# Other slot numbers in the order tables of a decoder layer (attention, eight experts, ternary layer) on one core

## The chip, the cores and the metric

The kernel runs on one core of a Trainium2 chip. The metric is the device time of the core in microseconds (us). Five engine programs run side by side and meet at semaphores: PE (TensorE, matmuls and transposes), DVE (VectorE), ACT (ScalarE), POOL (GpSimd) and SP (SyncE, which issues the DMAs). PEld in the profile is PE's weight loads. PE's clock has two levels, 1.2 and 2.4 GHz; the profile gives the granted clock as a share of full speed.

## The reference

Sixteen batches of 128 tokens with 256 features go through one post-norm layer (cut to what matters):

```
def attn(x):                       # 16 heads of 16
    scores = q k^T / 4, causal
    vals, idx = top_k(scores, 32)  # the 32 largest of each row stay
    return (softmax(masked scores) @ v) Wo^T + bo
def xattn(x, ctx, itok):           # 8 experts, 256 -> 512 -> 256
    h = relu(proj_in[e] @ x);  o = proj_out[e] @ h
    gate[b, s, e] = sum of ctx[b, s, k] where itok[b, s, k] == e
    return sum over e of gate[e] * o[e]
def ffn(x):                        # Hadamard, 4 bits, ternary weight
    return quantize4(x @ H) @ ternary(weight)^T
x = layernorm(x + attn(x)); x = layernorm(x + xattn(x)); x = layernorm(x + ffn(x))
```

## The kernel before, in words

**Units.** The work is cut into 8 units of 2 batches (256 tokens). Each unit passes through steps: q, k and v projections; four score tiles k = 0..3 (scores, copy_scores and exp, first_max, select, keep, turn_probs twice, copy_probs, attend, normalise; a tile is 8 heads of one batch); turn_o, copy_ot, out_proj; ln1_stats, rstd1, ln1_apply, turn_x1 and the two copies x1t_high and x1t_low; the 8 experts; the second layernorm, turn_x2, hadamard, quantise, turn_q4, ffn; the third layernorm and the store. Below, step.index@unit names one of them: L1.0.1@3 is the first expert matmul of expert 0, half 1, in unit 3.

**Experts.** Each is two products with weights and activations split into a high and a low 16-bit part, three matmuls a product. L1.e.z (line 752, 12 matmuls) computes half z of the 512 hidden values of expert e into ps_z; ACT's relu writes h_hi (line 576) and h_raw (line 580); POOL's h_low (line 462) is the difference of the two. L2.e.b (line 768, 12 matmuls) takes all hidden values of batch b, so it waits for h_low of both halves. ACT's gate_out scales the result and POOL's gated_add sums it up. PE's order of experts is L1.0.0, L1.0.1, L1.1.0, L2.0.0, L1.1.1, L2.0.1, and so on: the first L2 of an expert stands one L1 behind the second half of it.

**Weight preparation.** In the first unit each expert's weights are read from HBM (load_w, two buffers), squared and summed (w_squares on ACT, w_sum on PE at line 778), given a power-of-two scale by w_scale (DVE, lines 931 to 944), and split by w_high (ACT, lines 607 and 609) and w1_low and w2_low (POOL, lines 471 and 474). L1 and L2 of unit 0 wait for these.

**One bank.** q, k, v, attend, turn_o, out_proj, turn_x1, turn_x2, hadamard, turn_q4 and ffn all write the PSUM tile ps_misc; each waits (take_misc, table MISC) until the reader of the one before it in PE's order has read it. So which step waits for which reader follows from the order.

**The order.** It is written out by numbers. `build_schedule` gives each step of each unit a slot: unit v starts at 32 v, the steps of a tile have an offset from 8 k + shift_k, experts run one step a slot from `at["experts"]`. The steps are sorted by slot (ties stay in the order of placing), and `walk` lets each engine run its own steps in that order. Four tables hold the numbers: FIRST for unit 0, SECOND for unit 1, STEADY for units 2 to 6, LAST for unit 7; PREP and PREP_SLOTS place the weight preparation. The semaphore waits belong to the steps and go with them.

```
        at = FIRST if v == 0 else SECOND if v == 1 else LAST if v == UNITS - 1 else STEADY
        base = SLOTS * v
    return [step for _, step in sorted(placed, key=lambda x: x[0])]
```

As slots of unit v + 1 run from 32 (v + 1) and the experts of unit v from 32 v + 44, the score tiles and attends of the next unit lie among the experts of this one.

Of the kernel before, what the change touches and what calls it, by code (L numbers as in the profile page):

```python
# [111 lines left out]
}  # L112
FIRST = STEADY | {
    "experts": 42.5, "shift1": 1.5, "relu": 0.5, "gate_out": 3, "shift2": 0.5, "copy_ot": 38.5, "shift0": 3,
    "select": 3.75, "copy_scores": -3.75, "copy_v": 10.5, "shift3": -0.5, "out_proj": 40, "turn_probs2": 10.5,
    "gate_scale": 48.5, "gated_add": 2, "pace": 0.875, "x_plus_bo": 27, "scores": -3.75, "rstd2": 76.75, "v": 10,
    "keep": 6.5, "ffn_residual": 86.25, "ln2_stats": 77.5, "spread_q": -4.75, "rstd1": 38.25, "k": -6.25,
    "x2t_high": 77.75, "load_ctx": 20.25, "copy_probs": 8, "attend": 12.25, "gate_sums": 31.5, "turn_probs": 8.75,
# [914 lines left out]
```

How the kernel before makes its waits and increments, by code:

```python
        def wait(eng, s, value):  # L368
            if value > 0:
                eng.wait_ge(s, value)
# [4 lines left out]
        @block.sync  # L376
# [9 lines left out]
            def step(name, v, *args):  # L386
# [10 lines left out]
                        .then_inc(s_ctx, 16)  # L397
                    sp.dma_start(itok_sb[:, :, :], itok.rearrange("b s k -> s b k")[:, v * UB:(v + 1) * UB, :])\
                        .then_inc(s_ctx, 16)
                elif name == "load_w":
                    e, = args
                    wait(sp, w1_low_ready, e - STAGED + 1)
                    wait(sp, w2_low_ready, e - STAGED + 1)
                    sp.dma_start(w1_raw[:, e % STAGED, :, :], rows(w1t[e])).then_inc(w_loaded[e % STAGED], 16)
                    sp.dma_start(w2_raw[:, e % STAGED, :, :], rows(w2t[e])).then_inc(w_loaded[e % STAGED], 16)
                elif name == "store":
                    sp.wait_ge(out_ready, v + 1)
                    sp.dma_start(out.rearrange("b s d -> s b d")[:, v * UB:(v + 1) * UB, :], out_sb[:, :, :])\
                        .then_inc(s_store, 16)
            sp.dma_start(wq_sb[:, :, :], rows(wqt)).then_inc(s_qk, 16)
            load_xt(0)
# [6 lines left out]
            sp.dma_start(wo_sb[:, :, :], rows(wot)).then_inc(s_vo, 16)  # L419
            sp.dma_start(bv_sb[:, :], bv[:, :]).then_inc(s_vo, 16)
            sp.dma_start(bo_sb[:, :], bo.rearrange("(a n) -> a n", a=1).broadcast_to([P, D])).then_inc(s_vo, 16)
            sp.sem_inc(s_store, 16)
            walk("sp", step, sp)
            sp.wait_ge(s_store, 16 * (UNITS + 1))
```

## Time and profile before

| | |
|---|---|
| median of three runs | 622.8 us (622.05 to 624.53) |
| the profiled execution, own time | 624.53 us |
| its span, first to last instruction | 622.7 us |
| mean granted clock of PE | 0.941 |
| busy, share of the span | PE 89%, PEld 77%, DVE 77%, ACT 62%, POOL 55% |
| L1 and L2 matmuls (lines 752 and 768) | 3072 of PE's 7156 instructions, 273 to 274 ns each |

A row of a timeline has the start in us from the start of the span, the duration, the engine, the line, the operation with output and inputs, and in square brackets the idle time of the engine before it with what released it. Matmuls overlap (a new one starts every 0.11 us, each takes 0.27), so the ends of PE's rows are modelled. "<-issue" means that the profile shows nothing that was waited for. The rows themselves stand in a section of their own, in numbered groups.

### The profile page before, as it was taken

To read this page: it belongs to the slowest core of one execution; us is meant where nothing else is said; L and a number is where in the kernel's file an instruction comes from. 1 tells how busy PE (TensorE), PEld (TensorE's weight loads), DVE (VectorE), ACT (ScalarE), POOL (GpSimd) and SP (SyncE) were. 2 spreads that over 40 slices of the span, in tenths; PEclk is the share of its full clock that TensorE was granted. 3 is DMA by queue.
4 is the path that set the end of the run, shared out by engine and by line. 5 is a ranking of instruction groups with operands and counts; after the bars stand their busy time and mean duration, and the time that the engine had idled before them with its cause. 6 is when DMAs were issued, how large, how long until landed. Compare 5 with 4: busy or idle time off the path is not lost. (4 is left out here: it accounts for less than half of the span.)

```text
span 622.7 us, 20334 instructions
## 1 busy us (share of the span) xinstructions
PE 553.3 (89%) x7156; PEld 478.9 (77%) x7156; DVE 477.5 (77%) x2995; ACT 387.2 (62%) x909; POOL 344.3 (55%) x336
## 2 busy tenths in 40 slices
...
PEclk9568578999999999999999999999999999999985
...
GB/s 234 78 146 136 86 103 2 3 17 37 3 2 3 64 8 2 3 3 69 3 1 21 53 3 2 3 70 1 3 3 53 3 3 1 19 0 3 18 0 17
DMA packets 20021, 19.88 MB, mean 32 GB/s; under 512 B 1744, under 2 KB 17872, under 8 KB 19920
## 3 DMA queue, kind: packets, MB, share of 16 engines
...
HBM read 16.49 MB, written 2.10 MB: 30 GB/s over the span
## 5 line engine op out<-in xcount | busy, mean ns | idle before, releaser
L462 POOL TENSOR_TENSOR h_lo<-h_raw,h_hi 128x512 f16<-128x512 f32 x128 | 149.5, 1169 | 158.9 <-ACT h_raw L580 158.2
L768 PE MATMUL ps_o<-w_hi,h_lo 128*128 128x256 f16 x512 | 139.8, 273 | 4.3 <-POOL h_lo L462 3.1
L752 PE MATMUL ps_z<-x1t_hi,w_lo 128*128 128x256 f16 x512 | 140.5, 274 | 0.6 <-DVE x1t_lo L910 0.6
L752 PE MATMUL ps_z<-x1t_lo,w_hi 128*128 128x256 f16 x512 | 140.3, 274 | 0.0
L752 PE MATMUL ps_z<-x1t_hi,w_hi 128*128 128x256 f16 x512 | 140.3, 274 | 0.0
L768 PE MATMUL ps_o<-w_hi,h_hi 128*128 128x256 f16 x512 | 139.5, 273 | 0.0
L768 PE MATMUL ps_o<-w_lo,h_hi 128*128 128x256 f16 x512 | 139.5, 273 | 0.0
L854 DVE MATCH_REPLACE8 taken<-next,taken 128x48 f32<-128x48 f32 (+2 forms) x576 | 127.6, 233 | 0.2
L576 ACT ACTIVATE h_hi<-ps_z 128x512 f16<-128x512 f32 x128 | 75.9, 593 | 57.9 <-PE ps_z L752 57.0
L849 DVE MAX8 next<-taken 128x8 f32<-128x48 f32 (+2 forms) x576 | 95.9, 235 | 0.1
L483 POOL TENSOR_TENSOR acc<-go_sb,acc 128x512 f32<-128x512 f32 x56 | 71.2, 1271 | 36.4 <-ACT go_sb L590 36.2
L580 ACT ACTIVATE h_raw<-ps_z 128x512 f32<-128x512 f32 x128 | 76.0, 593 | 0.0
L590 ACT ACTIVATE go_sb<-ps_o,gate 128x256 f32<-128x256 f32 x128 | 53.7, 474 | 25.0 <-PE ps_o L768 24.9
L768 PEld LDWEIGHTS ps_o<-w_hi,h_lo 128*128 128x128 f16 x512 | 50.0, 98 | 13.2 <-POOL h_lo L462 5.2
L553 ACT ACTIVATE pt_sb<-ps_pt 64x512 f32<-64x512 f32 x64 | 38.0, 593 | 35.4 <-PE ps_pt L714 35.3
L752 PEld LDWEIGHTS ps_z<-x1t_hi,w_lo 128*128 128x128 f16 x512 | 50.4, 98 | 7.5 <-DVE x1t_lo L910 1.0
L768 PEld LDWEIGHTS ps_o<-w_lo,h_hi 128*128 128x128 f16 x512 | 50.1, 98 | 7.1
L752 PEld LDWEIGHTS ps_z<-x1t_lo,w_hi 128*128 128x128 f16 x512 | 50.4, 98 | 6.7
L752 PEld LDWEIGHTS ps_z<-x1t_hi,w_hi 128*128 128x128 f16 x512 | 50.4, 98 | 6.0
L768 PEld LDWEIGHTS ps_o<-w_hi,h_hi 128*128 128x128 f16 x512 | 50.1, 98 | 5.8
L545 ACT ACTIVATE ps_s<-s_sb,neg_max 128x48 f32<-128x48 f32 (+2 forms) x192 | 51.5, 317 | 0.0
L714 PE MATMUL ps_pt<-ident,p_sb 128*128 128x128 f32 x256 | 42.5, 292 | 9.5 <-DVE p_sb L863 5.7
...
## 6 DMA issues: line engine op xcount, KB each, us to landing
...
```

The costliest lines, as they stand in the source:

```text
L462: nc.gpsimd.tensor_tensor(h_lo[:, e % 2, 2 * z:2 * z + 2, :], h_raw[:, z, :, :], h_hi[:, e % 2, 2 * z:2 * z + 2, :], ALU.subtract)\
L483: nc.gpsimd.tensor_tensor(acc[:, :, :], go_sb[:, e % 2, :, :], prev[:, :, :], ALU.add)\
L545: last = act.activation(dst, s_sb[:, k % 2, score_at(j):score_at(j) + m], ACT.Exp, bias=neg_max[:, k % 2, j:j + 1], scale=SCALE)
L553: act.activation(pt_sb[0:rows, k % 2, :, HALF * half:HALF * (half + 1), :].rearrange("p h j q -> p j h q"), ps_pt[0:rows, :].rearrange("p ...
L576: act.activation(h_hi[:, e % 2, 2 * z:2 * z + 2, :], ps_z[z][:, :].rearrange("p (c t) -> p c t", c=2), ACT.Relu)\
L580: act.activation(h_raw[:, z, :, :], ps_z[z][:, :].rearrange("p (c t) -> p c t", c=2), ACT.Relu)\
L590: last = act.activation(go_sb[:, e % 2, b, :], ps_o[e % 2][:, b * D:(b + 1) * D], ACT.Copy, scale=gate[:, b, e:e + 1])
L714: last = pe.transpose(ps_pt[:, i * P:(i + 1) * P], p_sb[:, k % 2, at:at + P], ident[:, :])
L752: last = pe.matmul(ps_z[z][:, d * UT:(d + 1) * UT], w[:, e, c, at:at + P], x[:, c, :], start=n == 0, stop=n == len(terms) - 1)
L768: last = pe.matmul(ps_o[e % 2][:, b * D:(b + 1) * D], h[:, e % 2, c, b * SEQ:(b + 1) * SEQ], w[:, e, c, :], start=n == 0, stop=n == len(te ...
L849: last = V.max(next8[:, j, :], t)
L854: last = V.match_replace(t, next8[:, j, :], t, TAKEN)
```

## The change

Only numbers in the tables change, in all four of them and in PREP; PREP_SLOTS goes from 6.0 to 5.5. Every step, instruction, buffer and semaphore is the same, and so is the work of each engine. What changes is the order of the steps within PE, DVE, ACT, POOL and SP. Of the tables, some numbers:

```diff
 STEADY = {
-    "shift0": 1.25, "shift1": 0, "shift2": 1.5, "shift3": -1, "scores": -6.5, "copy_scores": -6.25, "exp": 5.25,
-    "select": 2, "pace": 1, "keep": 7.25, "turn_probs": 8.5, "copy_probs": 8.25, "turn_probs2": 10,
-    "copy_probs2": 9.75, "attend": 11.75, "normalise": 12.75, "load_xt": 10, "q": -14, "copy_q": -13.25,
...
+    "shift0": 1.25, "shift1": 0, "shift2": 1.5, "shift3": -0.75, "scores": -5.75, "copy_scores": -6, "exp": 5,
+    "select": 1.75, "pace": 1.625, "keep": 7.25, "turn_probs": 8.25, "copy_probs": 8, "turn_probs2": 9.25,
+    "copy_probs2": 8.75, "attend": 10.75, "normalise": 12.75, "load_xt": -0.25, "q": -12.75, "copy_q": -13.5,
...
-PREP_SLOTS = 6.0
+PREP_SLOTS = 5.5
 PREP = {
-    "load_w": 10.75, "w_squares": 0.25, "w_sum": 2.25, "w_scale": 3.75, "w_high": 3.5, "w1_low": 3.75, "w2_low": 5.5,
-    "ffn_abs": -6.25, "ffn_sum": 26, "ffn_ternary": 42.25,
+    "load_w": 2, "w_squares": -0.75, "w_sum": 1.5, "w_scale": 3, "w_high": 1.75, "w1_low": 6.5, "w2_low": 9.75,
+    "ffn_abs": 14.25, "ffn_sum": 19, "ffn_ternary": 43.5,
 }
```

What this does to the order is seen in three places. First PE in unit 3, at the first expert (units 2, 4 and 5 have the same rows; within a group of twelve matmuls only the first is shown). Before, with attend.0 of unit 4 (L725) behind L1.0.1 (ps_z1):

```order
L752 MATMUL ps_z0<-x1t_hi,w1_lo 128x256 [waits relu_done,x1t_low]
...
L752 MATMUL ps_z1<-x1t_hi,w1_lo 128x256 [waits relu_done]
...
L725 MATMUL ps_misc<-v_sb,pt_sb 64x17 [waits v_copied,pt_copied,x1t_low]
...
L752 MATMUL ps_z0<-x1t_hi,w1_lo 128x256 [waits relu_done]
...
L768 MATMUL ps_o0<-w2_hi,h_lo 128x256 [waits go_done,h_low_done]
```

And after:

```order
L752 MATMUL ps_z0<-x1t_hi,w1_lo 128x256 [waits relu_done,x1t_low]
...
L725 MATMUL ps_misc<-v_sb,pt_sb 64x17 [waits v_copied,pt_copied,x1t_low]
...
L752 MATMUL ps_z1<-x1t_hi,w1_lo 128x256 [waits relu_done]
...
L752 MATMUL ps_z0<-x1t_hi,w1_lo 128x256 [waits relu_done]
...
L768 MATMUL ps_o0<-w2_hi,h_lo 128x256 [waits go_done,h_low_done]
```

The attend moved from behind L1.0.1 to ahead of it, so only L1.0.1 and L1.1.0 are left between L1.0.1's start and L2.0.0.

Second PE in the start, where q@1 (L636) stands among the steps of unit 0 (L725 attend, L714 turn_probs, L778 w_sum, L695 scores). Before:

```order
L778 MATMUL ps_o0<-w_sq,ones 128x2 [waits w_step,w_squared]
L725 MATMUL ps_misc<-v_sb,pt_sb 64x17 [waits v_copied,pt_copied]
L725 MATMUL ps_misc<-v_sb,pt_sb 64x17 x15
L636 MATMUL ps_misc<-xt_sb,wq_sb 128x256 [waits xt_loaded,o_ready]
L636 MATMUL ps_misc<-xt_sb,wq_sb 128x256 x3
L714 MATMUL ps_pt<-ident,p_sb 128x128 [waits pt_copied,p_ready]
L714 MATMUL ps_pt<-ident,p_sb 128x128 x3
L695 MATMUL ps_s<-kt_sb,q_spread 32x16 [waits s_copied,s_zeroed,p_ready,spread_ready,k_copied]
```

And after:

```order
L778 MATMUL ps_o0<-w_sq,ones 128x2 [waits w_step,w_squared]
L725 MATMUL ps_misc<-v_sb,pt_sb 64x17 [waits v_copied,pt_copied]
L725 MATMUL ps_misc<-v_sb,pt_sb 64x17 x15
L714 MATMUL ps_pt<-ident,p_sb 128x128 [waits pt_copied,p_ready]
L714 MATMUL ps_pt<-ident,p_sb 128x128 x3
L636 MATMUL ps_misc<-xt_sb,wq_sb 128x256 [waits xt_loaded,o_ready]
L636 MATMUL ps_misc<-xt_sb,wq_sb 128x256 x3
L714 MATMUL ps_pt<-ident,p_sb 128x128 [waits pt_copied,p_ready]
L714 MATMUL ps_pt<-ident,p_sb 128x128 x3
L778 MATMUL ps_o0<-w_sq,ones 128x2 [waits w_step,w_squared]
L695 MATMUL ps_s<-kt_sb,q_spread 32x16 [waits s_copied,s_zeroed,p_ready,spread_ready,k_copied]
```

q@1 moved behind a turn_probs, and w_sum.3 stands ahead of scores.2@0 now, with q@1 before it.

Third POOL around rstd1@0 (L493, L496), with the weight blocks (L471, L474) of experts 5 and 6. Before:

```order
L474 TENSOR_TENSOR w2_lo<-w2_raw,w2_hi 128x1024 [waits w2_low_step]
L493 TENSOR_SCALAR var_eps<-meanvar 128x2 [waits stat_step0]
L496 TENSOR_TENSOR rstd<-var_eps,minus_half 128x2 [waits eps_added0]
L471 TENSOR_SCALAR w1_raw<-w1_raw,w_pow 128x1024 [waits w_high_ready]
L474 TENSOR_TENSOR w1_lo<-w1_raw,w1_hi 128x1024 [waits w1_low_step]
L471 TENSOR_SCALAR w2_raw<-w2_raw,w_pow 128x1024 [waits w_high_ready]
L474 TENSOR_TENSOR w2_lo<-w2_raw,w2_hi 128x1024 [waits w2_low_step]
L462 TENSOR_TENSOR h_lo<-h_raw,h_hi 128x512 [waits relu_done] x3
```

And after:

```order
L471 TENSOR_SCALAR w1_raw<-w1_raw,w_pow 128x1024 [waits w_high_ready]
L474 TENSOR_TENSOR w1_lo<-w1_raw,w1_hi 128x1024 [waits w1_low_step]
L493 TENSOR_SCALAR var_eps<-meanvar 128x2 [waits stat_step0]
L496 TENSOR_TENSOR rstd<-var_eps,minus_half 128x2 [waits eps_added0]
L462 TENSOR_TENSOR h_lo<-h_raw,h_hi 128x512 [waits relu_done] x3
L471 TENSOR_SCALAR w2_raw<-w2_raw,w_pow 128x1024 [waits w_high_ready]
L474 TENSOR_TENSOR w2_lo<-w2_raw,w2_hi 128x1024 [waits w2_low_step]
```

w1_low.6 stands ahead of rstd1@0 now, and three h_lows directly behind it, ahead of w2_low.6.

## Rows read from the trace of the kernel before

**Rows 1.** The page, busy times and clock in 40 slices of 15.6 us.

```profile
PE 553.3 (89%) x7156; PEld 478.9 (77%) x7156; DVE 477.5 (77%) x2995; ACT 387.2 (62%) x909; POOL 344.3 (55%) x336
...
PEclk9568578999999999999999999999999999999985
```

**Rows 2.** Windows: length, busy us (instructions), granted clock, DMA share, GB/s.

```profile
75.00:90.00 15.00, 8.39 (x92) 5.85 (x91) 12.72 (x73) 7.65 (x18) 7.49 (x7) 0.73 0.31 107
300.00:360.00 60.00, 59.51 (x761) 52.13 (x758) 51.30 (x323) 39.83 (x100) 33.56 (x36) 1.00 0.07 20
```

**Rows 3.** Waits of PE from 0 to 105 us: total, times, longest.

```profile
PE ps_o L778 <- ACT w_hi L602: 12.1, 6, 3.8
...
PE ps_misc L653 <- DVE x L817: 5.6, 1, 5.6
```

**Rows 4.** Timeline of PE at turn_x2 of unit 7.

```profile
604.67 1.09 PE L653 MATMUL ps_misc<-ident,x 128*128 128x128 f32 x4 [5.74 <-DVE x L817]
```

**Rows 5.** Timeline of PE at the first expert of unit 3.

```profile
297.70 0.27 PE L752 MATMUL ps_z<-x1t_hi,w_lo 128*128 128x256 f16 x1
...
299.10 1.11 PE L725 MATMUL ps_misc<-v_sb,pt_sb 128*64 128x17 f32 x32
300.15 0.28 PE L752 MATMUL ps_z<-x1t_hi,w_lo 128*128 128x256 f16 x1
...
301.58 0.28 PE L768 MATMUL ps_o<-w_hi,h_lo 128*128 128x256 f16 x1
```

**Rows 6.** Timelines of ACT and POOL at the same place.

```profile
299.21 0.60 ACT L576 ACTIVATE h_hi<-ps_z 128x512 f16<-128x512 f32 x1 [0.22 <-PE ps_z L752]
299.70 0.59 ACT L580 ACTIVATE h_raw<-ps_z 128x512 f32<-128x512 f32 x1
...
299.06 2.47 POOL L462 TENSOR_TENSOR h_lo<-h_raw,h_hi 128x512 f16<-128x512 f32 x2 [2.10 <-ACT h_raw L580]
```

**Rows 7.** Timeline of PE at the first expert of unit 7.

```profile
553.28 0.27 PE L752 MATMUL ps_z<-x1t_hi,w_lo 128*128 128x256 f16 x1
...
557.16 0.28 PE L768 MATMUL ps_o<-w_hi,h_lo 128*128 128x256 f16 x1 [1.06 <-POOL h_lo L462]
```

**Rows 8.** Timelines: holes of PE where one unit turns into the next, and keep.1@1.

```profile
107.14 0.82 DVE L863 SCALAR_TENSOR_TENSOR p_sb<-taken,ps_s 128x640 f32<-128x640 f32 x1
...
108.17 1.24 PE L695 MATMUL ps_s<-kt_sb,q_spread 32*32 32x16 f32 x64 [1.08 <-issue]
...
156.72 0.27 PE L768 MATMUL ps_o<-w_hi,h_lo 128*128 128x256 f16 x1 [1.14 <-issue]
...
158.88 0.63 PE L653 MATMUL ps_misc<-ident,x 128*128 128x128 f32 x4 [0.68 <-DVE x L817]
...
547.57 0.63 PE L653 MATMUL ps_misc<-ident,x 128*128 128x128 f32 x4 [1.63 <-DVE x L817]
```

**Rows 9.** Timeline of PE in the start: v of unit 0, q of unit 1, out_proj.

```profile
25.16 3.76 PE L645 MATMUL ps_misc<-wv_sb,xt_sb 128*128 128x256 f32 x8
...
38.73 3.78 PE L636 MATMUL ps_misc<-xt_sb,wq_sb 128*128 128x256 f32 x8 [0.63 <-DVE o_sb L874]
...
81.09 3.61 PE L645 MATMUL ps_misc<-wo_sb,ot_sb 128*128 128x256 f32 x8 [0.44 <-ACT ot_sb L562]
```

**Rows 10.** Waits of DVE from 30 to 95 us: total, times, longest.

```profile
DVE w_ms L931 <- PE ps_o L778: 0.8, 1, 0.8
```

**Rows 11.** Timelines at ln1_apply of unit 0 and of unit 3.

```profile
87.98 3.42 DVE L817 TENSOR_SCALAR x<-t,meanvar,rstd 128x256 f32<-128x256 f32 x2 [0.24 <-POOL rstd L496]
...
89.13 2.12 POOL L474 TENSOR_TENSOR w_lo<-w_raw,w_hi 128x1024 f16<-128x1024 f32 x1
...
91.55 1.09 PE L653 MATMUL ps_misc<-ident,x 128*128 128x128 f32 x4 [5.62 <-DVE x L817]
...
94.05 0.40 PE L752 MATMUL ps_z<-x1t_hi,w_lo 128*128 128x256 f16 x1 [0.56 <-DVE x1t_lo L910]
...
290.13 0.74 DVE L817 TENSOR_SCALAR x<-t,meanvar,rstd 128x256 f32<-128x256 f32 x2 [0.73 <-POOL rstd L496]
```

More of the change, by code:

```diff
@@ L112 @@
+    "spread_q": -11.5, "k": -10, "copy_k": -10, "v": 3.5, "copy_v": 2, "load_x": 41, "load_ctx": 11.75,
+    "x_plus_bo": 15, "gate_sums": 31.5, "turn_o": 36.5, "copy_ot": 37.25, "out_proj": 38, "ln1_stats": 40.25,
+    "rstd1": 38.75, "ln1_apply": 41.75, "turn_x1": 41.5, "x1t_high": 41, "x1t_low": 42.5, "gate_scale": 51,
+    "experts": 44, "relu": 0, "h_low": -0.5, "gate_out": 0.5, "gated_add": -1, "ln2_stats": 77, "rstd2": 76,
[3 rows of a table added]
 }
 FIRST = STEADY | {
-    "experts": 42.5, "shift1": 1.5, "relu": 0.5, "gate_out": 3, "shift2": 0.5, "copy_ot": 38.5, "shift0": 3,
@@ L115 @@
[L115 to L118, printed above, removed]
-    "ln1_stats": 41, "to_q4": 83.25, "x1t_low": 42, "load_xt": -7.75, "load_x": 27, "ln2_apply": 80.25,
@@ L122 @@
+    "ln1_stats": 37.75, "scores": -4.75, "load_xt": -22.5, "pace": 1.5, "load_ctx": 8, "shift2": 1, "out_proj": 39.25,
+    "rstd1": 39.75, "ln3_apply": 100.5, "rstd3": 96.25, "copy_v": 8, "quantise": 82.25, "x2t_low": 79.5,
+    "x2t_high": 79.5, "copy_k": -8, "ffn_scale": 88.25, "ln3_stats": 90.5, "rstd2": 76.25, "copy_q4t": 84.5,
+    "q": -14.25, "to_q4": 83, "store": 143, "copy_q": -10.5, "k": -9.5, "ffn_residual": 87, "gate_scale": 50,
 }
 SECOND = STEADY | {
[L124 removed]
@@ L125 @@
-    "shift1": 1.25, "turn_q4": 87, "h_low": -1, "copy_v": 4, "ln2_stats": 75.5, "ln3_stats": 94.75, "attend": 11.25,
-    "copy_q": -11, "copy_ot": 36.75, "keep": 6.25, "shift2": 0, "x2t_low": 79.75, "gate_sums": 28.75, "shift0": 1.75,
-    "gate_scale": 48.25, "load_x": 34, "store": 117.25, "load_ctx": 14, "ln1_apply": 40.5, "ln2_apply": 78.5,
-    "x2t_high": 79.5, "k": -8.5, "v": 4, "x_plus_bo": 21.25, "copy_q4t": 85, "x1t_low": 42.75, "copy_scores": -5.5,
-    "turn_x1": 41.25, "copy_k": -8.25, "exp": 4.75, "turn_probs2": 9.5, "gated_add": -2, "ffn_residual": 91.25,
```

29 lines of the change are left out of this document (14 added, 15 removed), and 10 rows, old and new, of tables (LAST, STEADY).

## The prediction

> **What bounds the kernel now.** I read the page's busy shares and forty slices first, then the windows, then the waits of TensorE (PE), and last single timelines. PE is busy for 553.3 of 622.7 us, and its granted clock is at the full level in every slice but the first seven and the last ones [rows 1]. The windows say where it is the limit: from 300 to 360 us PE is busy for 59.51 of 60 us, while VectorE (DVE) has 51.30, ScalarE (ACT) 39.83 and GpSimd (POOL) 33.56. From 75 to 90 us PE has only 8.39 of 15, at a mean clock of 0.73, and DVE 12.72 [rows 2]. So the span has three stages. Up to 94 us, where the first expert matmul starts, the selection chain on DVE and the weight chain (w_squares, w_sum, w_scale, w_high, w_low) set the time, with PE between them at mostly 1.2 GHz: PE waited there 12.1 us at w_sum and 5.62 us at turn_x1 of unit 0 [rows 3]. From about 105 to 600 us a microsecond of idle PE is a microsecond of the end, and there a reordering gains or loses exactly the holes that it closes or opens. The last 20 us are a chain through ln2 and ln3 of unit 7, with a PE wait of 5.74 us [rows 4]; the change leaves the order of those steps alone, so I carry them at nothing.
>
> **The change part by part.** No instruction is added or removed, so every term is a wait. In each I name a step as step.index@unit.
>
> *The first expert of units 2 to 5.* L2.0.0 waits for h_low of both halves of expert 0. From the start of L1.0.1 that path is fixed: in unit 3, L1.0.1 starts at 297.70, ACT takes its two passes from 299.21 to 300.29, POOL's pair of h_low ends at 301.53, and L2.0.0 starts at 301.58, which is 3.88 us after L1.0.1 [rows 5, 6]. In unit 7 it is again 3.88 us (553.28 to 557.16), with only L1.0.1 and L1.1.0 in between, and there PE stood idle for 1.06 us [rows 7]. In unit 3 nothing shows as idle, because attend (299.10, 1.11 us) lies in between too [rows 5]. The new table puts this attend ahead of L1.0.1. In unit 3 it holds PE from the end of L1.0.1 (twelve matmuls whose starts lie 0.11 us apart: 297.70 + 1.31 = 299.01) to 300.15, so 1.14 us. With the new order L1.0.1 starts 1.14 us later, L2.0.0 still 3.88 us after it, and no other work moves into the gap, since the next row on PE is L2.0.0 itself: +1.14 us a unit, shown as a PE idle of about 1.1 us as in unit 7. Four units (2 to 5) give +4.6 us. Unit 1 has 4.92 us there already, for another reason, so I give it +0.1; in units 0, 6 and 7 the order here stays. The bounds are 0 (if POOL or ACT turned out quicker once attend is out of the way; nothing in the rows says so) and +5.0 (1.26 us each, if the 0.12 us seam ahead of L2.0.0 of unit 3 isn't used up); I take 4.6, as unit 7 shows the very order with the very hole.
>
> *The turn from unit 0 to unit 1.* Three holes of before are here: 1.08 us ahead of scores.3@1 (it waits for the end of keep.1@1, DVE 107.14 + 0.82), 1.14 ahead of L2.7.1@0 and 0.68 at turn_x1@1 [rows 8]. With the new order out_proj@1 stands between L1.7.1@0 and L2.6.1@0, and turn_x1@1 behind L2.7.1@0 and a turn_probs, so 1.14 and 0.68 are covered; DVE comes out of the start about 3.9 us further ahead of PE (w_scale.7 lies before the experts now), so 1.08 is covered. New: turn_x1@1 waits some 0.25; L1.0.0@1 now has only a turn_probs and a scores (2.15 us, against 3.91) to cover the two copies of x1t, which leaves 0.65. Sum 0.9 - 2.9 = -2.0, and a w_sum in passing makes it -1.9 to -2.35; I take -2.1.
>
> *The turn from unit 6 to unit 7.* turn_x1@7 waited 1.63 us for ln1_apply [rows 8]. It stands one expert group (1.31 us) later now: 0.32 remain, and the L2.7.0 and L2.7.1 ahead of it wait some 0.45 for their h_low. Net -0.85, between -1.3 and 0. Smaller holes of the steady part (none over 0.35 us) add -0.3, between -0.8 and +0.5.
>
> *The start, until L1.0.0@0 (94.05 in before).* Four moves. (a) v@0 (3.76 us) goes ahead of scores.1@0 [rows 9]; select.1 of tile 0 starts later by the w_scale that waits for it, +0.55. (b) q@1 (3.78 us) goes behind a turn_probs and ahead of w_sum.3, whose w_scale.3 stands two selects earlier on DVE. DVE waits there 2.5 us with PE at 1.2 GHz and 1.0 at 2.4; normalise.1@0 adds 0 to 2.2. In before DVE waited for w_sum only once, 0.8 us, in all of 30 to 95 [rows 10]; that one goes. keep.3@0 then ends 1.1 (warm) to 4.3 us (cold) later, of which 1.3 us are absorbed, since copy_ot of before stood behind w_squares.6: out_proj@0 starts at 81.2 to 84.4 instead of 81.09 [rows 9]. (c) ln1_apply@0 took 3.42 us in before against 0.74 in unit 3, while POOL ran the 2.12 us subtraction of a weight block beside it; PE waited 5.62 for it and started turn_x1@0 at 91.55 [rows 3, 11]. In the new order rstd1@0 stands behind w1_low.6 and ahead of the h_lows, and first_max.1@1 no longer lies between ln1_stats and ln1_apply, so turn_x1@0 can start 2.8 us earlier after the same out_proj. (d) But scores.2@1, turn_probs, w_sum.7 and on DVE keep.0@1 and w_scale.7 (1 to 2.1 us) lie between turn_x1@0 and L1.0.0@0 now: L1.0.0@0 starts 9.0 us after the end of out_proj@0 (its start + 3.6 us), at 93.8 (warm), 95.4 (mixed) or 97.0 (cold). Against 94.05 that is -0.2 to +3.0. I take +0.8, between warm and mixed, since the slices of the start read 0.5 to 0.8, a mix of the two levels [rows 1].
>
> On (c) the row shows 3.42 us for work that takes 0.74 elsewhere, next to a POOL instruction. The Trainium skill, page "SBUF — State Buffer", section "SBUF: two separate sides", says that VectorE and GpSimd share a port pair as an exclusive lock, held for the whole instruction, with the loser blocked entirely. By that rule the whole stretch goes once no POOL block stands beside ln1_apply. The rows alone allow also that DVE was slow for its own reasons, and then the 2.7 us stay: L1.0.0@0 comes 2.7 us later and the total is 627.7 instead of 625.0. I take 0.74, the row of unit 3 [rows 11], and leave 627.7 to the upper part of the range.
>
> *Queues.* load_xt, load_x, load_ctx and store change places on SyncE's queue (load_x of a unit behind a store, a store behind the next load_ctx). Every one of them still lands units ahead of its reader, and the store of unit 7 is last as before: 0.
>
> **Sum.** +0.8 - 2.1 + 0.1 + 4.6 - 0.85 - 0.3 = +2.25 us. The profiled execution took 624.53 us with a span of 622.7, 1.8 us around it; with the change its own time would be 626.8. It is the slowest of the three runs, whose median is 622.8; on the median the forecast is 625.0.
>
> **The rivals.**
> *A, the start runs warm.* If PE works at 2.4 GHz during v@1 and out_proj@0 (half of 3.7 us each; turn_x1 reads 1.09 us in unit 0 and 0.63 in unit 1 [rows 8, 11]), out_proj ends some 4 us earlier, and L1.0.0@0 starts at 89 to 91: 4 us less than the 94.05, instead of 0.8 more. 625.0 - 0.8 - 4.0 = 620.2. For it: w_sum and transposes stand closer together in the new order, and the slice means of 0.5 to 0.8 show that the clock rose here again and again [rows 1]. Against: PE was busy for 56% of 75 to 90 us [rows 2], and the clock fell back each time.
> The Trainium skill, page "TensorE: Matmul & The Clock Gate", section "HAM oscillation — how this bites in real kernels", says that the engine is throttled by default and released by activity; the page speaks for the sign of this rival, that an order with PE's work closer together runs warmer, but it gives no number for this mix. The trace agrees in so far as the full level stands in all slices of the steady part, where PE is full, and not in the start [rows 1].
>
> *B, the start runs cold (slower).* One mechanism: q@1 at 1.2 GHz (3.78 us) sits ahead of w_sum.3, DVE waits 2.5 us at w_scale.3 and then behind normalise.1@0, keep.3@0 ends 4.3 us later, and L1.0.0@0 starts at 97.0. It decides from the point where DVE's waits in 30 to 75 us exceed the 1.3 us of slack by copy_ot. 625.0 - 0.8 + 3.0 = 627.2; with new holes of the steady part at their upper end 629.5. For it: q@1 ran cold in before [rows 9], and so did out_proj. Against: before's own 0.8 and its stretched w_scale go.
>
> *C, the hole of the first expert doesn't open.* If POOL and ACT gave h_low 1.2 us sooner (in unit 3 POOL's record reads 2.47 us for two of them), units 2 to 5 cost nothing: 625.0 - 4.6 = 620.4. Against: the 3.88 us repeats in units 3 and 7 to the hundredth, with and without attend in between [rows 5, 7].
>
> **How the numbers follow.** Chances: forecast 0.42 (own range 623.5 to 626.5), A 0.16, B 0.28, C 0.14. The forecast and B lie together at 623.5 to 629.5, A and C at 619.5 to 621.5. I leave out what A and C give together (616) and what lies over 629.5: the range is 619.8 to 629.5. A measurement of this kernel can tell 0.5%, 3.1 us, from no change: faster means under 619.7, slower over 625.9. Faster takes a third of A and of C and their overlap: 0.14. Slower takes most of B (0.24) and a quarter of the forecast (0.10): 0.34. The rest, 0.52, is no change.
>
> **What would show it.** Right: L2.0.0 of units 2 to 5 each with a PE idle of about 1.2 us released by POOL's h_low, the period of a unit up from about 66.2 to 67.3 us; no hole at L2.7.1@0; turn_x1@7 with 0.3 instead of 1.63; L1.0.0@0 between 93.8 and 97; DVE waiting at w_scale.3 for w_sum. Wrong: L1.0.0@0 under 92 (A) or over 96 (B), L2.0.0 without a wait (C), or a hole over 0.5 us in the steady part that isn't in this list, above all at hadamard or at turn_probs.

## The result, and the profile after

The changed kernel took 647.6 us (median of 4 runs, 645.7 to 651.9) against 623.6 for the kernel before: the ratio is 1.039, with a 95% interval of 1.035 to 1.043. The forecast was 625.0 with a range of 619.8 to 629.5, so some 22 us of loss weren't foreseen. The profiled execution took 647.04 us with a span of 645.2, against a span of 622.7 before.

First the page, busy times and granted clock in 40 slices, which answer to [rows 1]:

```profile
PE 561.0 (87%) x7156; PEld 483.8 (75%) x7156; DVE 489.5 (76%) x2995; ACT 389.2 (60%) x909; POOL 345.7 (54%) x336
...
PEclk9666569999999999979999899989999999999985
```

The instruction counts are the same. DVE, though, is busy for 12.0 us more with the same 2995 instructions (489.5 against 477.5), and PE for 7.7 us more, where the forecast took the work of each engine as unchanged. PE's clock, which stood at 9 through the whole steady part, now shows 7, 8 and 8 in three slices of it.

The same window of the steady part as in [rows 2]:

```profile
75.00:90.00 15.00, 7.30 (x20) 5.03 (x20) 11.69 (x88) 6.87 (x17) 3.25 (x3) 0.61 0.40 123
300.00:360.00 60.00, 55.86 (x807) 48.66 (x806) 51.75 (x321) 36.73 (x88) 30.97 (x32) 0.99 0.03 7
```

PE has lost its full occupation: 4.1 us of 60 are idle, where 0.5 were. The starts of L1.0.0, the first expert matmul of a unit, say when: 97.05 in unit 0 (94.05 before), 162.87 in unit 1 (162.90), 230.97 in unit 2 (230.12), 304.64 in unit 3 (296.39), 376.48 in unit 4 (362.61), 448.30 in unit 5 (428.80), 516.99 in unit 6 (494.44), 574.47 in unit 7 (551.97). So the start loses 3.0 us and the experts of unit 0 give them back; 0.9 is lost in unit 1, then 7.4, 5.6, 5.6 and 3.05 in units 2 to 5, and nothing from unit 6 on. That is the 22.5 us of the spans. The start itself varies between executions: in the profiles of six other kernels below with the changed order up to L1.0.0 of unit 0 it is at 98.2 to 99.9 us, and in two more with the order of before (b_gate31, b_turns) at 91.0 and 92.2. So the start costs more than these 3.0 us, some 6 in the mean of the profiles (98.7 against 92.4), and a difference of 2 us at L1.0.0 between two single profiles says nothing.

The waits of PE from 110 us to the end (total, times, longest) name the new one:

```profile
PE ps_misc L645 <- DVE o_sb L874: 12.2, 5, 3.1
PE ps_o L768 <- POOL h_lo L462: 8.5, 8, 1.1
PE ps_misc L653 <- DVE x L817: 8.4, 6, 5.7
```

The second row holds the holes that were forecast at L2.0.0; the first, which had no counterpart at all before, is v waiting for normalise.3 of the unit before its own (both write or read the one bank ps_misc). The wait comes once among the experts of each of units 1 to 5, with 1.02, 3.05, 3.04, 3.05 and 1.99 us. The timeline of PE at the first expert of unit 3, and at v among the experts of the same unit:

```profile
310.99 0.28 PE L768 MATMUL ps_o<-w_hi,h_lo 128*128 128x256 f16 x1 [1.10 <-POOL h_lo L462]
...
357.12 2.65 PE L645 MATMUL ps_misc<-wv_sb,xt_sb 128*128 128x256 f32 x8 [3.04 <-DVE o_sb L874]
```

The same v in the kernel before has no wait. In the changed kernel the two instructions of normalise.3 on DVE come straight after other DVE work, without a wait of their own, so it is DVE that is late:

```profile
344.97 1.89 PE L645 MATMUL ps_misc<-wv_sb,xt_sb 128*128 128x256 f32 x8
```

```profile
356.55 0.19 DVE L872 RECIPROCAL rsum<-ps_misc 128x8 f32<-128x8 f32 x1
356.77 0.29 DVE L874 TENSOR_TENSOR o_sb<-ps_misc,rsum 128x128 f32<-128x128 f32 x1
```

And why normalise.3 is late. The timeline of DVE and then of POOL over the two gate_sums of unit 4, of which only some of the sixteen instructions are shown:

```profile
344.58 0.29 DVE L895 SCALAR_TENSOR_TENSOR gate_part<-itok_sb,ctx_sb 128x128 bf16<-128x128 int32 x1
...
344.79 1.36 DVE L895 SCALAR_TENSOR_TENSOR gate_part<-itok_sb,ctx_sb 128x128 bf16<-128x128 int32 x1
...
346.08 1.23 DVE L895 SCALAR_TENSOR_TENSOR gate_part<-itok_sb,ctx_sb 128x128 bf16<-128x128 int32 x1
...
347.24 0.28 DVE L895 SCALAR_TENSOR_TENSOR gate_part<-itok_sb,ctx_sb 128x128 bf16<-128x128 int32 x1
...
348.73 1.23 DVE L895 SCALAR_TENSOR_TENSOR gate_part<-itok_sb,ctx_sb 128x128 bf16<-128x128 int32 x1
...
350.11 1.35 DVE L895 SCALAR_TENSOR_TENSOR gate_part<-itok_sb,ctx_sb 128x128 bf16<-128x128 int32 x1
...
351.81 1.23 DVE L895 SCALAR_TENSOR_TENSOR gate_part<-itok_sb,ctx_sb 128x128 bf16<-128x128 int32 x1
...
344.64 1.35 POOL L483 TENSOR_TENSOR acc<-go_sb,acc 128x512 f32<-128x512 f32 x1 [0.79 <-ACT go_sb L590]
345.96 1.20 POOL L462 TENSOR_TENSOR h_lo<-h_raw,h_hi 128x512 f16<-128x512 f32 x1
348.54 1.28 POOL L462 TENSOR_TENSOR h_lo<-h_raw,h_hi 128x512 f16<-128x512 f32 x1 [1.38 <-ACT h_raw L580]
350.04 1.27 POOL L483 TENSOR_TENSOR acc<-go_sb,acc 128x512 f32<-128x512 f32 x1 [0.22 <-ACT go_sb L590]
351.59 1.30 POOL L462 TENSOR_TENSOR h_lo<-h_raw,h_hi 128x512 f16<-128x512 f32 x1 [0.28 <-ACT h_raw L580]
```

Eleven of the sixteen instructions take 0.28 to 0.29 us and five take 1.23 to 1.36; there are five POOL instructions in this stretch, and each long one ends about 0.15 us after one of them (344.79 + 1.36 = 346.15 and 344.64 + 1.35 = 345.99, for one). A gate_sums takes 1.78 us when no POOL instruction meets it; these two take 3.81 and 4.74. In the kernel before, the two took 2.34 and 2.91 at this place in units 4 and 5. All 128 instructions of the line, before and after (busy, mean ns):

```profile
L895 DVE SCALAR_TENSOR_TENSOR gate_part<-itok_sb,ctx_sb 128x128 bf16<-128x128 int32 x128 | 40.8, 379 | 0.0
```

```profile
L895 DVE SCALAR_TENSOR_TENSOR gate_part<-itok_sb,ctx_sb 128x128 bf16<-128x128 int32 x128 | 56.7, 507 | 0.0
```

The Trainium skill states this on the page "SBUF — State Buffer", section "SBUF: two separate sides": a DVE operation with two SBUF inputs and a GpSimd operation that reads SBUF lock each other out of the port pair they share, for a whole instruction. The trace agrees: one POOL instruction, one blocked DVE instruction, of about the POOL instruction's length (1.36 us beside 1.35, 1.23 beside 1.20).

The hole also costs clock. Windows of four us at v (353.9 to 361.9 is the stretch of the hole, of v and of L1.6.1):

```profile
352.00:356.00 4.00, 2.08 (x48) 1.63 (x36) 3.83 (x25) 0.73 (x1) 0.89 (x1) 1.00 0.25 70
356.00:360.00 4.00, 2.88 (x11) 2.18 (x12) 3.87 (x32) 0.19 (x1) 0.00 (x0) 0.79 0.00 2
360.00:364.00 4.00, 4.00 (x30) 3.32 (x29) 4.00 (x32) 2.27 (x6) 0.70 (x1) 0.78 0.40 131
```

The granted clock falls from 2.4 GHz to 1.2 GHz for part of two windows after the idle 3 us. From start to start, v takes 2.44 us instead of 1.73, and L1.6.1 behind it 2.37 instead of 1.31. So a unit of 71.84 us instead of 66.22 is made of 1.14 (L2.0.0), 3.2 (the hole at v), 0.7 and 1.06 (the slow clock), less about 0.5 elsewhere, which wasn't looked into. In unit 2 the clock stays low for about twice as long (0.65 in the window from 282 to 286 us and 0.50 from 286 to 290), and there 7.4 us are lost instead of 5.6.

### The profile page after: what moved, and what is told of

It reads as the page before. It is cut to its first block and busy times, and to the rows that moved or that the text cites. A ratio compares the mean times of both kernels' runs of the same rounds, so it can differ in the third digit from the quotient of the medians.

```text
span 645.2 us, 20334 instructions
## 1 busy us (share of the span) xinstructions
PE 561.0 (87%) x7156; PEld 483.8 (75%) x7156; DVE 489.5 (76%) x2995; ACT 389.2 (60%) x909; POOL 345.7 (54%) x336
## 5 line engine op out<-in xcount | busy, mean ns | idle before, releaser
L768 PEld LDWEIGHTS ps_o<-w_hi,h_lo 128*128 128x128 f16 x512 | 50.0, 98 | 17.3 <-POOL h_lo L462 10.5
L590 ACT ACTIVATE go_sb<-ps_o,gate 128x256 f32<-128x256 f32 x128 | 53.4, 470 | 13.0 <-PE ps_o L768 12.8
L895 DVE SCALAR_TENSOR_TENSOR gate_part<-itok_sb,ctx_sb 128x128 bf16<-128x128 int32 x128 | 56.7, 507 | 0.0
L714 PE MATMUL ps_pt<-ident,p_sb 128*128 128x128 f32 x256 | 42.6, 293 | 12.7 <-DVE p_sb L863 9.5
```

Source lines behind the costliest of these rows:

```text
L590: last = act.activation(go_sb[:, e % 2, b, :], ps_o[e % 2][:, b * D:(b + 1) * D], ACT.Copy, scale=gate[:, b, e:e + 1])
L714: last = pe.transpose(ps_pt[:, i * P:(i + 1) * P], p_sb[:, k % 2, at:at + P], ident[:, :])
L768: last = pe.matmul(ps_o[e % 2][:, b * D:(b + 1) * D], h[:, e % 2, c, b * SEQ:(b + 1) * SEQ], w[:, e, c, :], start=n == 0, stop=n == len(te ...
L895: last = V.scalar_tensor_tensor(gate_part[:, b, e, :], itok_sb[:, b, :], float(e), ctx_sb[:, b, :], ALU.is_equal, ALU.mult, accum_out=gate ...
```

## The experiments

Times are medians; the kernel before ran at 622.7 to 623.3 us beside them. A name with a_ is the changed kernel with an edit, b_ the kernel before with an edit, m_ a mix of both. Ratios are to the kernel before, with 95% intervals.

| run | time | ratio |
|---|---|---|
| a_gate_one_input | 622.3 | 0.9999 (0.997 to 1.003) |
| a_gate30 | 634.8 | 1.020 (1.017 to 1.023) |
| a_attend0 | 647.0 | 1.038 (1.035 to 1.041) |
| b_gate31 | 636.3 | 1.023 (1.019 to 1.027) |
| b_gate_one_input | 619.9 | 0.996 (0.994 to 0.997) |
| b_gate31_one_input | 620.4 | 0.996 (0.994 to 0.998) |
| a_thin_add | 627.1 | 1.007 (1.005 to 1.008) |
| a_gate36 | 653.9 | 1.052 (1.049 to 1.055) |
| a_two_back | 654.7 | 1.052 (1.048 to 1.055) |
| a_gate30_two_back | 634.2 | 1.017 (1.013 to 1.022) |
| a_one_input_unit0 | 642.5 | 1.031 (1.028 to 1.034) |
| b_late_gate | 635.3 | 1.021 (1.019 to 1.023) |
| b_late_gate_ctx | 628.9 | 1.011 (1.008 to 1.014) |
| m_late_gate | 642.9 | 1.031 (1.027 to 1.034) |
| b_turns | 622.8 | 1.000 (0.998 to 1.002) |

**Is it the blocking, or the order?** Same order, one input less. The multiplication with ctx is left out, so the gates are counts and the layer isn't computed; the same holds for every run below with one input.

```diff
-                        last = V.scalar_tensor_tensor(gate_part[:, b, e, :], itok_sb[:, b, :], float(e),
-                                                      ctx_sb[:, b, :], ALU.is_equal, ALU.mult,
-                                                      accum_out=gate_raw[:, b, e:e + 1])
+                        last = V.tensor_scalar(gate_part[:, b, e, :], itok_sb[:, b, :], float(e), 0.0,
+                                               ALU.is_equal, ALU.add, accum_out=gate_raw[:, b, e:e + 1])
```

> The changed kernel with the same order, but each gate_sums instruction reads only the index tile (the multiplication with ctx is left out, so the gates are counts). Theory 1: what blocks a gate_sums instruction is that it reads two tiles of SBUF while POOL works; with one input all sixteen take their 1.8 us or so a batch at any place, the hole at v goes (3.05 us and 1.8 us of slow clock behind it, in four to five units): about 627 us. If any DVE instruction is held up by POOL, the two gate_sums stay at 3.8 and 4.75 us and the time at 647. Theory 2: the hole stays at 2 us or more, time over 640.

Measured 622.3 us, 5 less than expected. The whole loss is gone. The line in this kernel, with the same 128 x 128 elements an instruction (the name of the operation is that of the one-input form):

```profile
L895 DVE TENSOR_SCALAR_CACHE_REDUCE gate_part<-itok_sb 128x128 bf16<-128x128 int32 x128 | 27.1, 280 | 0.0
```

Its mean is 280 ns, and each gate_sums takes 1.73 us wherever POOL works. The holes at v are gone, and of the waits of PE from 110 to 600 us only the one that was forecast has holes over 0.4 us:

```profile
PE ps_o L768 <- POOL h_lo L462: 8.8, 9, 1.1
```

The partner, the kernel before with the same edit:

> The kernel before with gate_sums reading only the index tile (no multiplication with ctx). It gives the like-for-like partner of the changed order with one input (622.3 us). If the rest of the prediction's sum holds (start +0.8, turn of units 0 and 1 -2.1, first expert +4.6, turn of units 6 and 7 -0.85), this is about 620 us; the holes of the steady part are as before and the period stays 66.2 us, since gate_sums hides no PE there. If contention held PE up in the kernel before too, it is 615 or less.

Measured 619.9 us, against 622.3 for the changed order: without the blocking the change costs 2.4 us, where the sum said 2.25. The intervals of the two ratios, 0.994 to 0.997 and 0.997 to 1.003, touch, so the size is good to about 2 us only; the two profiled executions differ by 0.2 us (spans 619.5 and 619.7). In before the blocking had a small price too, some 2.8 us. A unit takes 65.8 to 65.9 us there in units 2 to 4 and not the 66.2 that the expectation kept.

**Which number of the table does it?** In the changed kernel gate_sums went back to its old slot, with the place of unit 0 kept:

```diff
-    "x_plus_bo": 15, "gate_sums": 31.5, "turn_o": 36.5, "copy_ot": 37.25, "out_proj": 38, "ln1_stats": 40.25,
+    "x_plus_bo": 15, "gate_sums": 30, "turn_o": 36.5, "copy_ot": 37.25, "out_proj": 38, "ln1_stats": 40.25,
```

> The changed kernel with one number back: gate_sums at slot 30 in STEADY (units 2 to 6), 31.5 kept in unit 0. Theory 1, contention: in the changed kernel the two gate_sums of a unit take 3.8 and 4.75 us against 1.78 when no POOL instruction runs beside them, and that delay makes v of the next unit wait 3.05 us for normalise.3. With gate_sums.0 ahead of normalise.2 and keep.3 again other POOL work meets them; if they fall back to about 2.3 and 2.9 us the hole at v goes and with it the slow PE clock behind it: 647 - 4 x 4.5 = about 629 us, hole at v under 1 us. Theory 2, order alone: DVE has the same work ahead of normalise.3 in either place, so the hole at v stays at 3 us and the time at 645 to 647 us.

Measured 634.8, 6 us over what was expected: 12.8 of the 24 us come back. In units 4 and 5 the gate_sums now take 1.78 and 2.79 us (one long instruction of sixteen), and the holes at v are gone. What is left is the start, where gate_sums keeps its new place, holes of 0.4 to 1.8 us at turn_probs, which waits for keep (5.1 us in 6), and the holes at L2.0.0.

The reverse, one number of the change in the kernel before:

```diff
-    "x_plus_bo": 23.75, "gate_sums": 30, "turn_o": 36, "copy_ot": 35.5, "out_proj": 38.25, "ln1_stats": 40.25,
+    "x_plus_bo": 23.75, "gate_sums": 31.5, "turn_o": 36, "copy_ot": 35.5, "out_proj": 38.25, "ln1_stats": 40.25,
```

> The kernel before with one number of the change: gate_sums at slot 31.5 in STEADY, so that the two stand together behind keep.3. Theory 1: it depends on what POOL does then; the two stretch by 1 to 3 us, but v of the next unit stands 1.3 us later behind attend.3 and DVE is 5 us ahead there: 0 to +1 us a unit, 623 to 627. If this one number carries most of the loss: 635 to 645.

Measured 636.3, so +13.6 us from one number: the second case of the expectation, and far over the 0 to 1 us a unit that theory 1 was given. The waits of PE from 110 to 600 us in this kernel:

```profile
PE ps_misc L645 <- DVE o_sb L874: 13.3, 5, 2.8
```

It moves gate_sums.0 behind normalise.2 and keep.3, so that the two stand together, and then four POOL instructions meet them: 3.80 and 3.79 us in unit 4. But the move could also do harm by leaving DVE idle where gate_sums.0 stood before. To tell these apart, the same number with one input:

> The kernel before with gate_sums at 31.5 in STEADY (636.3 us with both inputs) and gate_sums reading one input. In the two-input run the hole at v was 2.8 us a unit, while the gate_sums took 3.81 and 3.79 us against 2.34 and 2.91 in before. If contention is the cause, one input (1.73 each, 4.1 us less) closes the hole and the time is that of before with one input, 620 us. If the cause is that keep.3 and normalise.2 no longer wait behind gate_sums (DVE's idle time isn't filled any more), a hole of 0.5 us or more stays and the time is over 623.

Measured 620.4, that of its partner without the moved number (619.9). The move costs nothing that can be told with one input, and 13.6 us with two. The idle time of DVE doesn't matter here; the blocking does.

**Dose.** POOL's gated_add of experts 1 to 7 on 8 of 256 columns, which leaves out the rest of that sum:

```diff
-                    nc.gpsimd.tensor_tensor(acc[:, :, :], go_sb[:, e % 2, :, :], prev[:, :, :], ALU.add)\
+                    w = D if e == 0 else 8
+                    nc.gpsimd.tensor_tensor(acc[:, :, :w], go_sb[:, e % 2, :, :w], prev[:, :, :w], ALU.add)\
```

> The changed kernel with POOL's gated_add of experts 1 to 7 done on 8 of 256 columns (the rest of the sum is left out), gate_sums with both inputs. Dose test of theory 1: two of the five POOL instructions that meet gate_sums (gated_add.3 and .4) become short, the three h_lows stay. Gate_sums from 3.8 and 4.75 to about 2.8 and 3.8 us, the hole at v from 3.05 to about 1.1 us and no slow clock behind it: 628 to 634 us. If DVE slows down by POOL's work in general and not by one blocked instruction per POOL instruction, the durations of single gate_sums instructions spread between 0.28 and 1.3; I expect only values near 0.28 and near the length of the POOL instruction.

Measured 627.1, just under the 628 to 634 that were expected. A short POOL instruction costs DVE 0.02 us, a long one about its length. At 338.46 and 342.36 POOL starts these two:

```profile
338.46 0.30 POOL L484 TENSOR_TENSOR acc<-go_sb,acc 128x16 f32<-128x16 f32 x1 [0.79 <-ACT go_sb L591]
...
342.36 1.30 POOL L462 TENSOR_TENSOR h_lo<-h_raw,h_hi 128x512 f16<-128x512 f32 x1 [1.78 <-ACT h_raw L581]
```

and on DVE the instructions beside them read:

```profile
338.61 0.30 DVE L896 SCALAR_TENSOR_TENSOR gate_part<-itok_sb,ctx_sb 128x128 bf16<-128x128 int32 x1
...
342.57 1.23 DVE L896 SCALAR_TENSOR_TENSOR gate_part<-itok_sb,ctx_sb 128x128 bf16<-128x128 int32 x1
```

The gate_sums take 2.76 and 2.73 us (expected 2.8 and 3.8; a third h_low no longer meets them, since they end sooner), and no hole is left at v (expected 1.1).

**The start.** One input in unit 0 alone, in the changed kernel (here too the layer isn't computed in full):

> The changed kernel with one-input gate_sums in unit 0 alone. There the two took 4.5 to 5.4 and 2.7 to 3.7 us beside the weight preparation on POOL, against 1.73 each. The first expert matmul starts 4 to 6 us earlier (92 to 94 instead of 97 to 99 us) if DVE's chain sets it. Of the total 1 to 5 us come through: 642 to 646; the holes at v in units 2 to 6 stay at 3 us.

Measured 642.5, so about 5 us of the 24 lie here. L1.0.0 starts at 92.78 instead of 97.05 (97.1 to 99.9 over the seven profiles with two inputs). In the changed kernel gate_sums of unit 0 meets the weight blocks, which are POOL's longest instructions:

```profile
69.03 2.20 DVE L895 SCALAR_TENSOR_TENSOR gate_part<-itok_sb,ctx_sb 128x128 bf16<-128x128 int32 x1
...
72.66 2.21 DVE L895 SCALAR_TENSOR_TENSOR gate_part<-itok_sb,ctx_sb 128x128 bf16<-128x128 int32 x1
```

The two together take 8.2 us there, 4.3 in before and 3.4 with one input.

**The forecast hole of the first expert.** In the changed kernel attend.0 went back behind L1.0.1 in units 2 to 6:

```diff
-                put(tile + at[name], engine, name, v, k)
+                put(tile + at[name] + (name == "attend" and k == 0 and 1 < v < 7), engine, name, v, k)
```

> The changed kernel with attend.0 of units 2 to 6 one slot later, so behind L1.0.1 as before, nothing else moved. By the prediction's own term the hole of 1.10 us at L2.0.0 in units 1 to 5 goes (five units, 1.14 us each): 5 to 6 us less, about 642. If the hole only moves on into the later wait at v (DVE is late there, not PE), the hole at v grows from 3.05 to about 4.2 us and the time stays at 647.

Measured 647.0, no change. The time is that of the second expectation, but the holes fit neither: the one at v stayed at 3.0 to 3.1 us, and the one at L2.0.0 went from 1.10 to 0.75 only. The timeline of POOL says why:

```profile
308.11 1.16 POOL L462 TENSOR_TENSOR h_lo<-h_raw,h_hi 128x512 f16<-128x512 f32 x1 [1.62 <-ACT h_raw L580]
309.24 0.22 POOL L493 TENSOR_SCALAR var_eps<-meanvar 128x2 f32<-128x2 f32 x1
309.54 0.71 POOL L496 TENSOR_TENSOR rstd<-var_eps,minus_half 128x2 f32<-128x2 f32 x1
310.21 1.15 POOL L462 TENSOR_TENSOR h_lo<-h_raw,h_hi 128x512 f16<-128x512 f32 x1
```

rstd2 stands between the two h_lows in the new order. A second move of the change had put another step of about 1 us into the same path, hidden as long as the first hole was there. So both went back, attend.0 by the edit above and rstd2 by this one, with gate_sums at 30:

```diff
-    "experts": 44, "relu": 0, "h_low": -0.5, "gate_out": 0.5, "gated_add": -1, "ln2_stats": 77, "rstd2": 76,
+    "experts": 44, "relu": 0, "h_low": -0.5, "gate_out": 0.5, "gated_add": -1, "ln2_stats": 77, "rstd2": 77,
```

> The changed kernel with gate_sums at 30 in STEADY (634.8 us), and attend.0 and rstd2 back to their places of before in units 2 to 6. Without the hole at v the 1.10 us holes at L2.0.0 are the limit there: if the prediction's term is right, it is 5 us less, 629 to 630, and the holes at L2.0.0 are gone. If they only move on (DVE late elsewhere), 634 to 635.

Measured 634.2 against 634.8. The holes at L2.0.0 of units 2 to 5 are gone, and new ones of 0.57 to 0.69 us stand at turn_x2, which waits for ln2_apply, that is for DVE and for rstd2. The hole moved on. As an amount to be won back from the full change, the forecast's 4.6 us isn't there; as a difference of two orders without blocking it is, since with one input units 2 to 5 are 1.0 to 1.5 us longer each in the changed order (66.4 to 67.4 against 65.3 to 65.9), 4.7 together.

**Past the deadline.** gate_sums at 36, behind normalise.3, and then the same with attend.0 and rstd2 back:

```diff
-    "x_plus_bo": 15, "gate_sums": 31.5, "turn_o": 36.5, "copy_ot": 37.25, "out_proj": 38, "ln1_stats": 40.25,
+    "x_plus_bo": 15, "gate_sums": 36, "turn_o": 36.5, "copy_ot": 37.25, "out_proj": 38, "ln1_stats": 40.25,
```

> The changed kernel with gate_sums at slot 36 in STEADY (units 2 to 6; 31.5 kept in unit 0): on DVE both gate_sums of a unit now stand behind normalise.3, so v of the next unit does not wait for them, blocked by POOL or not. Theory 1 says that the loss is their time ahead of normalise.3: no hole at v, PE clock full, about 624 us (the changed order with one-input gate_sums took 622.3), with the holes of 1.10 us at L2.0.0 left. If something else of the new order makes DVE late, a hole over 1 us stays in the steady part and the time is over 632.

> As the run with gate_sums at 36, and besides attend.0 of units 2 to 6 one slot later (behind L1.0.1) and rstd2 at 77, so that on POOL it stands behind h_low.0.1. In the run with attend.0 alone a hole of 0.75 us was left at L2.0.0, because rstd2 (1.01 us) stood ahead of h_low.0.1 on POOL. With both back the hole should go: 5 x 1.1 = 5 us less than with gate_sums at 36 alone, 618 to 620 us, which would beat the kernel before. If another wait takes its place (hole at L2.0.0 over 0.5 us or a new one at turn_x2), the two are within 1 us of each other.

Measured 653.9 and 654.7: slower still. The 624 and the 618 to 620 us that were hoped for didn't come; in both it was the other case of the expectation, another wait in its place. The hole at v did go. But DVE then stood idle for 3.2 us ahead of normalise.3, and gate_sums came after that and pushed ln1_apply back. The waits of PE from 110 to 600 us in the first of the two:

```profile
PE ps_misc L654 <- DVE x L818: 16.7, 6, 5.0
```

Each unit has two places where PE waits for DVE soon, v behind normalise.3 and turn_x1 behind ln1_apply, and the work between them must fit into DVE's idle time as well as onto its queue.

**Trying to take gate_sums off the start.** In the kernel before, gate_sums of unit 0 behind ffn_ternary, where PE already runs experts:

```diff
-    "x2t_high": 77.75, "load_ctx": 20.25, "copy_probs": 8, "attend": 12.25, "gate_sums": 31.5, "turn_probs": 8.75,
+    "x2t_high": 77.75, "load_ctx": 20.25, "copy_probs": 8, "attend": 12.25, "gate_sums": 43.5, "turn_probs": 8.75,
```

> The kernel before with one number changed: gate_sums of unit 0 at 43.5, so on DVE behind ffn_ternary, after x1t_low, where PE already runs experts. It takes 4.3 us of DVE work (2.54 + 1.78) off the chain ahead of the first expert matmul. If that chain is DVE's, L1.0.0 of unit 0 starts 2 to 4 us earlier and the time is 619 to 621; if PE or the weight chain sets it, 622 to 623.

Measured 635.3, where 619 to 623 was expected. L1.0.0 started at 92.15. That is earlier than the 94.05 of before, but b_gate31 and b_turns, whose order up to there is that of before, started at 91.0 and 92.2, so a gain at the start isn't shown. And then PE waited, in the window from 92 to 125 us:

```profile
PE ps_o L778 <- ACT w_hi L602: 10.6, 1, 10.6
```

On SyncE's queue load_ctx of unit 1 waits until gate_sums of unit 0 has read its buffer, and load_w of expert 7 stands behind it. With load_ctx of unit 1 at 16, behind that load_w:

```diff
-    "gate_scale": 48.25, "load_x": 34, "store": 117.25, "load_ctx": 14, "ln1_apply": 40.5, "ln2_apply": 78.5,
+    "gate_scale": 48.25, "load_x": 34, "store": 117.25, "load_ctx": 16, "ln1_apply": 40.5, "ln2_apply": 78.5,
```

> The kernel before with gate_sums of unit 0 at 43.5 as in the earlier run (635 us), and load_ctx of unit 1 at 16 instead of 14, so that on SyncE's queue it stands behind load_w of expert 7. In the earlier run PE waited 10.6 us at w_sum.7 for w_squares.7, whose weights stood behind a load_ctx that waited for gate_sums. If that is the whole loss, 622 to 624 us: first expert matmul at 92, and the hole at scores.3 of unit 1 larger by the 1.5 to 3 us that DVE is behind. If DVE's lateness is the loss, over 630.

Measured 628.9, between the two cases of the expectation: the 10.6 us wait is gone, but L2.0.0 of unit 0 now waits 5.0 us for w_scale.7, which is behind gate_sums on DVE. The queue was half of the loss (6.4 us of 12.6), and the rest goes with DVE. A mix, with the tables of the change for units 0 and 1 and the preparation and those of before for the rest, and gate_sums of unit 0 at 43.5, was slower still:

> A mix: the tables of the change for units 0, 1 and the weight preparation, those of before for units 2 to 7, and gate_sums of unit 0 at 43.5. The changed start reached L1.0.0 of unit 1 at 157.4 us with one-input gate_sums against 162.9 in before, so without the blocked gate_sums of unit 0 (4.53 + 3.7 us) most of these 5 us should be had with both inputs: 617 to 620 us. If the gain was the one-input arithmetic elsewhere, 622 to 624.

Measured 642.9, where 617 to 620 was expected, with holes of 3.11 us at scores.3 of unit 1 and of 2.2 to 2.9 us at v and at L2 matmuls of units 0 to 2. Why it loses so much where it goes from one table to another wasn't looked into further.

**Only the turns.** The kernel before with the moves at the two turns to which the prediction gave a gain:

```diff
-    "turn_x1": 41.25, "copy_k": -8.25,
+    "turn_x1": 41.75, "out_proj": 38.75, "copy_k": -8.25,
...
-    "copy_q": -14.25, "turn_x1": 40.5,
+    "copy_q": -14.25, "turn_x1": 41.25,
```

> The kernel before with three numbers: out_proj of unit 1 behind L1.7.1 (38.75), turn_x1 of unit 1 behind L2.7.1 (41.75), turn_x1 of unit 7 behind L2.6.1 (41.25). These are the moves of the change at the two turns that the prediction gave -2 and -0.85 us. Holes of 1.14, 0.68 and 1.63 us should shrink to about 0, 0.3 and 0.35: 620 to 621 us, ratio 0.996. If the waits only pass on to L1.0.0 (x1t_low) or L2.7.0 (h_low), 622.5.

Measured 622.8, ratio 1.000. The holes shrank from 1.14 + 0.68 to 0.69 at L2.7.0 and 0.50 at L1.0.0 of unit 1, and from 1.63 to 0.32 at turn_x1 and 0.52 at L1.0.0 of unit 7. A new one of 0.29 us stands at L2.7.0 of unit 6. That is 1.1 us less idle time by the trace, too little to be told from times that spread from 620.9 to 624.4 us. No run that computes the layer in full was faster than the kernel before.

## Why the prediction was wrong, point by point

**The step that failed** is the first sentence of the part on the change: "No instruction is added or removed, so every term is a wait." It took the durations of the kernel before as given under any order. They are not: one line on DVE went from 379 to 507 ns in the mean, because the new order puts it beside POOL's work, and through normalise.3 that reached PE among the experts of five units. The prediction had the rule in its hands. It weighed the blocking of DVE by POOL for ln1_apply of unit 0 [rows 11], and applied it to that one step rather than asking which lines of DVE read two SBUF tiles and what stands beside them in the new order. gate_sums is the step that the runs point to. In before its two parts stood beside POOL instructions for 0.7 and 1.5 us in unit 4; in the new order for 2.6 and 3.85. The row of the line, 379 ns in the mean where an undisturbed one reads 280, was there to be seen and isn't in any group of rows.

**The steady part** was called free of new holes but for L2.0.0. The largest was missing: 3.05 us at v, with 1.8 us of slow clock behind it. With blocking left out of both orders, this statement holds (no hole over 0.4 us beside L2.0.0), so the order of steps was read rightly and the durations weren't.

**The first expert, +4.6:** the mechanism and the size were right: holes of 1.10 us at L2.0.0 in units 1 to 5, where unit 7 shows 1.06 [rows 7], with L2.0.0 3.89 us after L1.0.1 in unit 3. Without blocking units 2 to 5 are 4.7 us longer. What was missed is rstd2, which would hold 0.75 us of each hole open by itself (a_attend0). Unit 1, given +0.1, has 1.10 in place of 0.99. Unit 6, where the prediction said that the order stays, has 0.81 that before had not: rstd2 stands between the two h_lows there too, ahead of the second.

**The turn from unit 0 to 1, -2.1:** the holes of [rows 8] at scores.3 of unit 1, at L2.7.0 of unit 0 (the prediction calls it L2.7.1) and at turn_x1 of unit 1 are all closed, and L1.0.0 of unit 1 doesn't wait. From L1.0.0 of unit 0 to that of unit 1 it is 65.8 us instead of 68.9: -3.0, and -3.35 with one input. The term had the right sign and mechanism and was small by about one us.

**The turn from unit 6 to 7, -0.85:** turn_x1 of unit 7 was to wait 0.32 and waited 1.33. From L1.0.0 of unit 6 to that of unit 7 nothing was gained (57.48 us against 57.52), and 0.55 with one input, where turn_x1 waits 0.34. In the changed kernel ln1_apply was stretched, as in the start of before:

```profile
569.57 1.67 DVE L817 TENSOR_SCALAR x<-t,meanvar,rstd 128x256 f32<-128x256 f32 x2 [1.45 <-POOL rstd L496]
```

It reads one large SBUF tile and is blocked nonetheless (0.73 to 0.74 elsewhere), beside an h_low that runs from 569.94 to 571.09. No run leaves out this blocking alone.

**The start, +0.8, and rival B:** L1.0.0 started at 97.05, the very number of rival B, but not by its mechanism. DVE's waits for w_sum between 30 and 98 us sum up to 1.6 us and not 2.5 at w_scale.3 alone. With one-input gate_sums in unit 0 they are longer (2.7 us from 30 to 75), and still the start is at 92.78. A rival that hits its number isn't thereby confirmed, and that it hit it is chance: the other profiles with this start are at 98.2 to 99.9. What failed in the forecast's own +0.8 is the start of out_proj: 84.68, over its 81.2 to 84.4, as gate_sums of unit 0 takes 8.2 us in place of 4.3; with one input in every unit out_proj starts at 80.92 and L1.0.0 at 92.37. Term (c) was right: ln1_apply of unit 0 took 0.73 us.

```profile
91.17 0.73 DVE L817 TENSOR_SCALAR x<-t,meanvar,rstd 128x256 f32<-128x256 f32 x2 [1.37 <-POOL rstd L496]
...
92.05 1.09 PE L653 MATMUL ps_misc<-ident,x 128*128 128x128 f32 x4 [4.16 <-DVE x L817]
```

turn_x1 came 7.4 us after the start of out_proj, where it was 10.5 before, and started at 92.05 all the same. Rival A didn't come about: out_proj took 3.21 us, against 3.61 before. (The words of the Trainium skill, page "TensorE: Matmul & The Clock Gate", on which that rival draws, that the default state is throttled and activity releases the throttle, stand there in the section "What's actually happening" and not in the one that the prediction names.) Rival C was wrong: the hole opened.

**The sum.** With the blocking taken out of both kernels the difference is 2.4 us, give or take 2, against a forecast of 2.25. That they agree so well is luck. By the two profiles with one input, the start is -0.9 (forecast +0.8), the turn from unit 0 to 1 -3.35 (-2.1), units 2 to 5 +4.7 (+4.6) and the turn from unit 6 to 7 -0.55 (-0.85), which is about 0. The steady part was forecast well, the start and the turns to within 1 to 2 us, and the missing term, some 21 us, was about nine times the whole sum.
